# Row maxima turned by VectorE over a DRAM buffer, and layer norm applied by GpSimd, in a fused two-block transformer kernel

## What is computed

```
x = x + L0_attention(layernorm(x))     # 16 heads of 8 columns, biases on q, k, v
x = x + L0_ffn(layernorm(x))           # silu(gate) * up, 384 hidden, then down
x = x + L1_attention(layernorm(x))     # 16 heads of 8, rms norm on each head's q and k
x = x + L1_ffn(layernorm(x))           # dense 128x128 + 8 experts of rank 8, softmax gates in bf16
layernorm(x) = (x - mean) / sqrt(var + 1e-5)
```

## Time and profile before

| | |
|---|---|
| median of 3 runs (lowest, highest) | 2131.88 us (2129.2, 2137.05) |
| profiled execution: time, span | 2135.92 us, 2134.1 us |
| PE busy | 1831.3 us, 86% |
| DVE busy | 1598.7 us, 75% |
| ACT busy | 1432.2 us, 67% |
| POOL busy | 432.8 us, 20% |
| mean granted TensorE clock | 0.934 of full speed |

### The profile page before, as it was taken

One profiled execution on the slowest core, in us unless ns is written; L12 is line 12 of the kernel. 1 busy time (PEld: TensorE's weight loads), 2 busy tenths in 40 slices (PEclk: granted clock), 3 DMA queues, 4 the chain that ended last, 5 costly groups with the idle time before them and its releaser, 6 DMA issues.

```text
span 2134.1 us, 38850 instructions
## 1 busy us (share of the span) xinstructions
PE 1831.3 (86%) x10958; PEld 688.9 (32%) x10958; DVE 1598.7 (75%) x3593; ACT 1432.2 (67%) x2921; POOL 432.8 (20%) x570
## 2 busy tenths in 40 slices
PE   4858989888988988888898888989898998998775
PEld 1232323333332333333333333323333332333322
DVE  4538888887878778778787878777787878888471
ACT  2716686776767677677766767676776768776543
POOL 2112131221212122121212212120121213121200
PEclk9957999999999999999999999999999999999867
DMA  5203223050413205041320504123050413212020
GB/s 109 71 11 101 47 67 96 18 140 17 118 34 96 65 17 140 17 115 37 81 81 17 140 17 115 36 71 91 17 140 17 115 37 79 79 35 59 29 53 16
DMA packets 162647, 140.87 MB, mean 66 GB/s; under 512 B 38761, under 2 KB 144050, under 8 KB 162482
## 3 DMA queue, kind: packets, MB, share of 16 engines
q1 hardware_dynamic: 162482, 139.29, 24.7%
HBM read 77.38 MB, written 55.57 MB: 62 GB/s over the span
## 4 chain that ended last, share of the span: by engine, by line
PE 37%; issue 24%; DMA 11%; ACT 9%; POOL 8%; DVE 8%; SPq 3%; ACTq 0%; POOLq 0%; DVEq 0%
PE ps L1127 11%; PE ps L1112 7%; PE ps L1148 5%; ACT probs L647 5%; DVE neg_max L853 4%; PE ps L1102 4%; DMA k_stack<-k_rows 4%; DMA rden_all<-rden_rows 3%; PE ps L1078 3%; PE ps L1153 2%; PE ps L1191 2%; DMA k_rows<-kp 2%; PE ps L1141 2%; POOL o_raw L551 2%; POOL qk L561 2%
## 5 line engine op out<-in xcount | busy, mean ns | idle before, releaser
L853 DVE TENSOR_REDUCE neg_max<-ps 128x1 f32<-128x512 f32 x2048 | 1316.4, 680 | 196.8 <-PE ps L1102 167.7
L647 ACT ACTIVATE probs<-ps 128x512 f32<-128x512 f32 x2048 | 1093.4, 599 | 324.5 <-PE ps L1112 309.0
L1102 PE MATMUL ps<-k_stack,q_stack 48*128 48x512 bf16 x2048 | 702.5, 402 | 86.6 <-DVE neg_max L853 46.4
L1112 PE MATMUL ps<-q_stack,k_stack 50*128 50x512 bf16 x2048 | 655.1, 391 | 79.8 <-ACT probs L647 75.7
L1127 PE MATMUL ps<-probs,v_aug 128*32 128x512 f32 x4096 | 568.1, 628 | 1.0
L1112 PEld LDWEIGHTS ps<-q_stack,k_stack 50*128 50x128 bf16 x2048 | 150.8, 95 | 525.1 <-ACT probs L647 342.4
L1102 PEld LDWEIGHTS ps<-k_stack,q_stack 48*128 48x128 bf16 x2048 | 159.3, 94 | 280.3 <-DVE neg_max L853 239.4
L551 POOL TENSOR_TENSOR o_raw<-o_raw,rden_all 128x512 f32<-128x512 f32 x64 | 81.3, 1270 | 569.6 <-DMA rden_all<-rden_rows 569.6
L1127 PEld LDWEIGHTS ps<-probs,v_aug 128*32 128x32 f32 x4096 | 81.7, 109 | 136.3 <-issue 81.5
L1153 PE MATMUL ps<-wo,o_raw 128*128 128x128 f32 x512 | 81.8, 326 | 43.2 <-POOL o_raw L551 43.1
L653 ACT ACTIVATE xn<-x,shift,rstd 128x128 f32<-128x128 f32 x192 | 80.5, 484 | 52.4 <-POOL shift L534 52.4
(11 more groups left out here) (103 smaller groups left out, 1499.4 us busy)
## 6 DMA issues: line engine op xcount, KB each, us to landing
q_stack<-q_rows SPq DMA_DIRECT2D x128, 192.0 KB, 3.7
k_stack<-k_rows SPq DMA_DIRECT2D x128, 192.0 KB, 4.6
rden_all<-rden_rows SPq DMA_DIRECT2D x64, 256.0 KB
q_rows<-qp SPq DMA_DIRECT2D x32, 384.0 KB, 2.6
k_rows<-kp SPq DMA_DIRECT2D x32, 384.0 KB, 2.9
q_rows<-qp SPq DMA_DIRECT2D x32, 256.0 KB, 3.0
k_rows<-kp SPq DMA_DIRECT2D x32, 256.0 KB, 3.0
x_in<-in_L_attn_x SPq DMA_DIRECT2D x16, 256.0 KB, 2.8
```

Source lines behind the costliest of these rows:

```text
L647: act.activation(probs[:, u % RING, :], ps[:, bank_of(l, u), :], ACT.Exp).then_inc(exps, 1)
L853: dve.tensor_reduce(neg_max[l][:, pair // 2, col:col + 1], ps[:, BANKS + bank_of(l, n), :], AX.X, ALU.max, negate=True).then_inc(max_taken, 1)
L1102: pe.matmul(ps[:, BANKS + bank_of(l, m), :], q_stack[l][row:row + KROWS, pair, tok:tok + 128], k_stack[l][row:row + KROWS, pair, :], start ...
L1112: pe.matmul(ps[:, bank_of(l, u), :], k_stack[l][row:row + AROWS, pair, tok:tok + 128], q_stack[l][row:row + AROWS, pair, :], start=True, s ...
```

## The change

1. The maxima's transposes leave PE and ACT. DVE writes the two bf16 parts into `m_parts` (now 128x32 bf16), and turns it in 32x32 blocks (`parts_turn`, one half step after `parts_low`) into `m_turned`. Within each block of 32 partitions the 32 columns (16 of each parity half: 8 high and 8 low parts) lie on the partitions. SP writes it to a DRAM buffer `m_rows` (8 KB), waits for that write (`m_out`), and then issues two DMAs that read the rows in the order that `q_stack` wants (64 runs of 64 bytes each). The pieces `m..` and `take_max` are gone, and with them the wait of the next piece for `gen`.
2. Layer norm's variance + eps, the shift (mean x rstd) and the application to four 128x128 tiles run on POOL (`norm_factors`, `apply_norm`: x*rstd - shift). DVE's `factors_in` and ACT's `apply_norm` are gone.

```diff
-X_PE = ((1, "xt0"), (3, "q0"), (4, "m01"), (5, "k0"), (7, "qt"), (8, "kt"), (11, "pr1"), (12, "m02"), (14, "v1"),
-        (19, "xt3"), (20, "m03"), (21, "rt"), (27, "ct"), (28, "m10"), (29, "out"))
+X_PE = ((1, "xt0"), (3, "q0"), (5, "k0"), (7, "qt"), (8, "kt"), (11, "pr1"), (14, "v1"),
+        (19, "xt3"), (21, "rt"), (27, "ct"), (29, "out"))
...
+        m_rows = [nc.dram_tensor(f"m_rows{l}", (4, 128, 32), BF16).ap() for l in (0, 1)]
...
             def max_rows(l, quarter, b):
 
-                hold(read[f"m{l}"], 4 * b + quarter + 1)
+                hold(turn_done[l], 4 * b + quarter + 1)
+                sp.dma_start(m_rows[l][quarter], m_turned[l][:, quarter, :]).then_inc(m_out[l], 16)
+                hold(m_out[l], 16 * (4 * b + quarter + 1))
                 for e in (0, 1):
                     sp.dma_start(q_stack[l][HALF * e + KROWS:HALF * e + AROWS, 2 * quarter:2 * quarter + 2, :],
-                                 m_parts[l][quarter % 2][16 * e:16 * e + 16, :]).then_inc(m_in[l][quarter], 16)
+                                 bass.AP(m_rows[l].tensor, (128 * quarter + 16 * e) * 32,
+                                         [[8 * 32, MROWS], [32, 8], [32 * 32, 4], [1, 32]])
+                                 ).then_inc(m_in[l][quarter], 16)
...
             def norm_factors(k, b):
 
+                wait_apart(pool, mv_done[k], b + 1, passed)
+                pool.tensor_scalar(vpe[k][:, :], mv[k][:, :, 1], LN_EPS, None, ALU.add).then_inc(var_ready[k], 1)
                 pool.wait_ge(var_ready[k], b + 1)
                 pool.tensor_tensor(rstd[k][:, :], vpe[k][:, :], half_neg[:, :], ALU.pow).then_inc(rstd_ready[k], 1)
                 pool.wait_ge(rstd_ready[k], b + 1)
-                pool.tensor_tensor(shift[k][:, :], neg_mean[k][:, :], rstd[k][:, :], ALU.mult).then_inc(shift_ready[k], 1)
+                pool.tensor_tensor(shift[k][:, :], mv[k][:, :, 0], rstd[k][:, :], ALU.mult).then_inc(shift_ready[k], 1)
+
+            def apply_norm(k, x, b):
...
+                for t in range(TT):
+                    last = pool.tensor_scalar(xn[k][:, t, :], x[:, t, :], rstd[k][:, t:t + 1], shift[k][:, t:t + 1],
+                                              ALU.mult, ALU.subtract)
+                last.then_inc(xn_ready[k], 1)
...
+            def parts_turn(l, quarter, b):
+
+                dve.wait_ge(low_done, 4 * maxima_before(l, b) + quarter + 1)
+                need(dve, m_in[l][quarter], 32 * b)
+                dve.transpose(m_turned[l][:, quarter, :], m_parts[l][:, quarter, :]).then_inc(turn_done[l], 1)
```

More of the change, by code:

```diff
@@ L202, in build @@
         rstd = [sb(f"rstd{k}", [128, TT]) for k in range(4)]
-        neg_mean = [sb(f"neg_mean{k}", [128, TT]) for k in range(4)]
         shift = [sb(f"shift{k}", [128, TT]) for k in range(4)]
@@ L294, in build @@
         high_done = sem("high_done")
-        low_done = [sem(f"low_done{l}") for l in (0, 1)]
+        low_done = sem("low_done")
+        m_out = [sem(f"m_out{l}") for l in (0, 1)]
+        turn_done = [sem(f"turn_done{l}") for l in (0, 1)]
         m_in = [[sem(f"m_in{l}{q}") for q in range(4)] for l in (0, 1)]
@@ L647, in exp_unit @@
                 act.activation(probs[:, u % RING, :], ps[:, bank_of(l, u), :], ACT.Exp).then_inc(exps, 1)
-            def apply_norm(k, x, tiles, b):
-                act.wait_ge(shift_ready[k], b + 1)
-                for t in tiles:
-                    last = act.activation(xn[k][:, t, :], x[:, t, :], ACT.Identity, bias=shift[k][:, t:t + 1],
-                                          scale=rstd[k][:, t:t + 1])
-                if tiles[-1] == TT - 1:
-                    last.then_inc(xn_ready[k], 1)
             def save_out(l, half, b):
@@ L685, in take_part1 @@
                 copy(qp[l][n][:, 1, :], qf[l][n][:, :]).then_inc(part1[2 * l + n], 1)
-            def take_max(l, quarter, b):
-                act.wait_ge(written[f"m{l}"], 4 * b + quarter + 1)
-                if quarter < 2:
-                    need(act, m_in[l][quarter + 2], 32 * b)
-                else:
-                    act.wait_ge(m_in[l][quarter - 2], 32 * (b + 1))
-                copy(m_parts[l][quarter % 2][:, :], gen[0:32, 0:128]).then_inc(read[f"m{l}"], 1)
             def gate_tanh(c, b):
@@ L721, in slot @@
                     act.wait_ge(bq_ready, 1)
-                    apply_norm(0, x_in, range(TT), 0)
                     take("xt0", xnt[0][:, :], 0)
@@ L728, in slot @@
                     weights_out()
-                    apply_norm(0, x_in, range(TT), 1)
-                    take_max(0, 0, 0)
                     return
@@ L740, in slot @@
                         exp_unit(0 if kind == "X" else 1, 2 * s + 1, i if kind == "X" else i - 1)
-                    for at_step, name in slot_pieces(kind, at):
-                        if at_step == s and name[0] == "m":
-                            take_max(int(name[1]), int(name[2]), i + PIECE[name][0])
                     if kind == "X":
@@ L773, in slot @@
                     else:
-                        if "S0" in have and s in (21, 22):
-                            apply_norm(0, x_in, (2 * s - 42, 2 * s - 41), i + 2)
                         if "M1" in have:
-                            if s == 12:
-                                apply_norm(1, x1, range(TT), i)
                             if s == 13:
@@ L1000, in slot @@
                             parts_low(l, step // 8 - 1, b)
+                        if work in have and e == 1 and step % 8 == 0 and 0 < step <= STEPS:
+                            parts_turn(l, step // 8 - 1, b)
                     if kind == "X":
@@ L1172, in piece @@
                     last = by_token(gen4, xnt[2], wqkv[:, 256:384], (2 * k, 2 * k + 1))
-                elif name[0] == "m":
-                    l, quarter = int(name[1]), int(name[2])
-                    pe.wait_ge(low_done[l], 4 * b + quarter + 1)
-                    last = turn(gen[0:32, 0:128], neg_max[l][:, quarter, :])
                 elif name in ("pr0", "pr1"):
```

57 lines of the change are left out of this document (27 added, 30 removed), and 2 rows, old and new, of the table PIECE.

## The result

The changed kernel takes 2316.01 us (median of 4 runs, 2303.53 to 2331.8) against 2132.68 of the kernel before in the same session: ratio 1.0862, 95% interval 1.0793 to 1.0932. It is 183 us slower. The forecast was 2154 with a range up to 2206: the sign was right, the size was not, and the time lies above the range. The profiled execution took 2316.5 us (span 2314.7), at a mean granted TensorE clock of 0.872 of full speed, 0.934 before.

The account below looks back on a forecast made before the run. It took a PE stream, 86% busy, to be held up at a few places by chains over other engines. Terms summed to -1.5 us per pair, times 15 = 22.5 us slower: 2154 us, range 2103 to 2206.

Parts of the forecast that it names:

- Step 4: Layer norm on POOL: 0.4 us per instruction, 1.6 us per norm, hidden by 1.9 us of slack; nothing gained or lost.
- rival C: POOL becomes a bound: instruction 1.26 us, norms 1 and 3 some 3 us late, 5 us per pair, about 2229; chance 0.06.
- Step 6: PE's clock: new stalls at units 32 and 48 bring about one more low-clock stretch, -0.7 us per pair, ends 0 and 1.7.
- Step 5: SP's extra DRAM leg for the maxima delays three places per pair of slots, by 1.3, 1.9 and 0.9 us.
- Units 32 and 38: Slot X: unit 32 waits 2.2 us, but the later stack decides at unit 38: -1.3 us per pair, ends 0.7 and 2.5.
- Unit 48: Slot X: the maxima's write lands behind layer 0's parts, -1.9 us per pair, ends 0 and 2.5.
- `pr0`: Slot Y: reciprocals issued at 1094.8 in place of 1094.09, -0.9 us per pair, ends 0.4 and 1.7.
- Steps 1 and 2: Relief per pair: transposes off PE give 1.9 us (ends 0.8, 3.8), ACT's lost work 1.2 us (ends 0, 2.5).
- Step 3: DVE loses two small norm instructions, gains 128 transposes of 0.17 to 0.35 us; +0.2 us per pair, ends -0.3 and +0.5.
- rival A: Faster: relief wins, small write not held behind layer 0's parts; +3.3 us per pair, about 2082, half relief 2105; chance 0.24.

Follow-up runs that it names:

- n2: Kernel before with layer norm's factors and application on POOL, written with mult and add, maxima the old way: 2130.65 us, ratio 0.9941.
- n1: Whole change with POOL's norm written with mult and add instead of mult and subtract, POOL negating the mean first: 2226.67 us, ratio 1.0395.
- e2: Kernel before with layer norm's factors and application on POOL as in the change, maxima the old way: 2239.91 us, ratio 1.048.
- e7: Kernel before with DVE applying layer norms 1 and 2: 2152.73 us, ratio 1.0086.
- n13: Kernel before plus only the maxima's DRAM leg, in the change's layout of 64-byte pieces; transposes and copies stay on PE and ACT: 2251.44 us, ratio 1.0507.
- e1: Changed kernel with layer norm put back as before; maxima go the new way by DVE and DRAM: 2225.06 us, ratio 1.043.
- n12: e1 with PE transposing and ACT copying a spare tile, results unused, at the eight old places: 2234.32 us, ratio 1.0429.
- n5: Kernel before with 128 extra DVE transposes of a spare tile, results unused: 2133.48 us, ratio 1.002.
- n7: n1 with SP's order changed as in e4: 2172.04 us, ratio 1.0181.
- e4: e1 with SP reordered in slot X: quarter 2's write ahead of the k parts, layer 0's parts behind quarter 3's maxima: 2170.88 us, ratio 1.0163.
- n11: n4 with SP's order changed as in e4: 2161.53 us, ratio 1.0174.
- e6: Kernel before with POOL applying layer norms 1 and 2 alone, with mult and add, factors on DVE: 2153.69 us, ratio 1.0082.
- n4: Kernel before plus only the maxima's DRAM leg, in 256-byte rows; transposes and copies stay on PE and ACT: 2185.66 us, ratio 1.0214.

## Why the prediction was wrong

**Step 4 failed by its price.** I took 0.4 us for POOL's instruction, because "it has one full input instead of two", from the 407 ns of a product. It measured 795. The subtraction was in the diff, no row of before showed POOL subtracting by a per-partition factor, and my far end, 1.26 us, was kept for rival C with a chance of 0.06. Had the instruction been written with mult and add it would have taken 448 ns and the step would have been nearly right: n2 waits 1.7 us per pair for `xn`, where the step had nothing, and still gains 0.6%, with 62.0 us of waits on ACT over the span instead of 75.7. Rival C priced 1.26 us at 5 us per pair; 795 ns alone cost 6 to 8 (after against n1, e2 against n2). So its mechanism, norms late on the path, was the right one for about half of the loss, though it named norms 1 and 3 and the waits are at norms 1 and 2. The Trainium skill (GPSIMD Engine Reference, "Engine selection") puts one-input elementwise work on GpSimd at roughly line rate. For this form with mult and add, VectorE took 344 ns (e7) and GpSimd 448 (n2), which bears that out only roughly; with a subtraction, at 795, the trace does not.

**Step 6 failed by its size, and its reading was too simple.** I let the new stalls at units 32 and 48 bring one more low stretch per pair and took 0.7 us for it. In n13, which has the change's leg and nothing else, a pair has 8.4 us more at 1.2 GHz and 2.9 us more busy time; in the whole change it is 18.1 us more and 7.8 us of slower matmuls. The step generalised from one row, 1100 to 1104, and the 3.4 us of its sum stands in none of the rows (the 16 matmuls of that row took 3.68). The same pair spoke against it: after the 1.72 us for `k_stack` the granted clock stayed at full speed (kernel before, columns as in the earlier trace rows):

```profile
1064.03:1068.03 4.00, 3.78 (x28) 1.41 (x32) 2.71 (x5) 3.05 (x8) 0.00 (x0) 1.00 1.13 270
```

**Step 5, place by place.** Its sum for the three places, 1.3 + 1.9 + 0.9 = 4.1 us, is near the 3.6 us by which n13's idle time grows, but that is partly luck, since no place has its size. *Units 32 and 38:* unit 32's own wait was right (median 2.1 us). The step then let the stack decide at unit 38, so that only 1.3 us would be lost. The stack's DMAs were late as said, but PE hardly waited for them: its wait for `k_stack` fell from 1.75 us per pair to 0.14 in after. PE came later than the step had it, as it ran on at the lower clock behind unit 32 (rows 1024 to 1032). Taken together the two waits grew by 0.6 us in after and 0.9 in n13; the rest of what the place costs is the slower matmuls, which belong to step 6. *Unit 48:* in after the write did stand behind the parts' data, its pair came 5.9 us after it. But PE was late by its other stalls and waited 0.56 us in that pair, 0.9 on average over the 13 pairs and 1.0 in n13, half of the 1.9. *`pr0`:* the reciprocals go out 4.05 us after `parts_low` in place of 3.59, and the wait is 1.86 instead of 1.34: 0.5, at the lower half of its ends; in n13 it grows by 0.8.

The write landed in 1.4 us at the median. The Trainium skill's 2 us for a DMA (DMA: Bandwidth & Descriptors, "Anatomy of one DMA — SWDGE (gpsimd) path"), given for GpSimd's queue, would have been further off for it, though the sum by it, 2172, was nearer. What the step left out is the layout: it took the pair's issue as 1.3 us, which is right for the change's 64-byte pieces, and did not see that reads from DRAM in rows of 256 bytes take 0.5.

**Steps 1 and 2, the relief, were too large.** 3.1 us per pair were forecast. e1 has all of it but the norms and is 9 us faster than n12 and 26 than n13, which is 0.6 to 1.7 us per pair, with intervals that overlap. PE's wait on ACT did not fall but rose, to 97 us in e1 and 104.7 after; why was not tested. In n2, without the new way of the maxima, it fell to 62.0.

**Step 3 was right**: 202 ns, and in n5 128 of them cost nothing clear of the noise.

**The range.** Its fast end, 2105, does not come out of its terms: half of rival A's relief is 2.5 us, less 1.7 is 0.8 us per pair, or 2120. It bears on nothing here, since the time lies above the other end.

So of the 183 us, some 90 to 100 are the subtraction (after against n1), some 45 to 55 the leg's place on SP (n1 against n7), in the same waits that the 64-byte pieces lengthen, and some 40 are what n7 keeps.

**Open.** e4, n7 and n11 still lose 1.6 to 1.8%, with PE's waits on `q_stack` gone. What their traces have more of is in the table's last column: over the span, PE's waits on ACT's exponentials and DVE's maxima together are 165 us in e4, 148 in n7 and 133 in n11, against 122 before, while the 24 us ahead of the maxima's transposes are gone from e4 and n7. Why they grow was not tested. All three also have the other order on SP, with the parts of layer 0 later, and no run has that order without the leg; so part of this loss can be the order's own. Nor was it settled why norms 1 and 2 on POOL with DVE's factors (e6) lose 0.8% while all four with POOL's factors (n2) gain 0.6%; PE's wait for `o_raw` is 0.7 us per pair longer in e6 than before, and not in n2. A version with both cures, the order and a 256-byte layout, could not have the transposes on VectorE in 32x32 blocks as they are, and was not tried.

## What to carry to other kernels

Price the instruction as it is written, operation included: where no row shows the exact form, measure the form, or keep the far end in the sum. In a stream that is held at a few points, a new stall can cost up to twice its length, when PE runs on at the lower clock behind it. Against before, a pair grew by 1.0 times the growth of its idle time in n4, 1.4 in e1, 1.8 in n13 and 2.0 in after, so keep both ends in the sum. Give a relief elsewhere little. When a small transfer takes another way, look at the size of its pieces and at what is ahead of it in its queue before its latency.
